# A one-core ViT block with a mixture of experts: the token step rearranged, scatters behind the normalising, four adds under way

## The reference

```python
h = einsum('bnd,ed->bne', patches(x), W) + b             # 768 -> 192
q, k, v = split(LN(h) @ W_attn + b_attn)                 # 12 heads of 16, rotary q and k
h = h + softmax(causal(q k^T / 4)) v @ W_proj + b_proj   # over the 16 tokens of an image
z = LN(h)
t = z * rsqrt(mean(z * z) + 1e-5) * norm_scale           # rmsnorm of the layer-normed row
g = t @ gate_w.T + gate_b                                # 16 experts, the best 4
w = softmax(top4(g))
y = sum over the 4: w_e * (swiglu(t @ W1_e + b1_e) @ W2_e + b2_e)   # inner width 384
return h + z + y
```

## Time and profile before

| what | value |
| --- | --- |
| device time, three runs | 524.96 us median (522.0 to 531.15) |
| profiled execution | 521.43 us, its span 519.6 us |
| PE busy in the span | 437.7 us (84%) |
| ACT, DVE, POOL busy | 311.0, 303.9, 257.2 us |
| mean granted clock of TensorE | 0.927 |
| moved by DMA | 49.73 MB, mean 96 GB/s |

### The profile page before, as it was taken

How to read it: one execution, slowest core, us unless ns; L and a number is a source line. 1 busy time by engine, 2 the same in 40 slices (tenths; PEclk the granted TensorE clock), 3 DMA queues, 4 the chain that set the end, 5 groups by cost and what they waited for, 6 DMA issues and landing times. The chain is left out here.

```text
span 519.6 us, 14443 instructions
## 1 busy us (share of the span) xinstructions
PE 437.7 (84%) x3867; PEld 388.2 (75%) x3868; DVE 303.9 (58%) x1048; ACT 311.0 (60%) x832; POOL 257.2 (50%) x302
## 2 busy tenths in 40 slices
PE   3788887797777758339999999999999999999970
PEld 2666765675566546229999999999999999999970
DVE  0466977878787666614555555555555555555550
ACT  1257656666665563217776767677766767777730
POOL 1124476667676666730334445345453644454443
PEclk9899999989999775559999999999999999999995
DMA  7995554555565111223333534434434443342332
GB/s 213 218 228 163 148 159 146 151 169 159 169 179 154 54 50 50 77 87 96 49 49 50 83 57 73 68 56 64 63 56 64 64 64 58 55 65 32 32 32 23
DMA packets 42107, 49.73 MB, mean 96 GB/s; under 512 B 6387, under 2 KB 33507, under 8 KB 42052
## 3 DMA queue, kind: packets, MB, share of 16 engines
q1 hardware_dynamic: 27604, 34.35, 25.2%
q0 software_dynamic: 14448, 14.72, 18.6%
HBM read 30.82 MB, written 18.23 MB: 94 GB/s over the span
## 5 line engine op out<-in xcount | busy, mean ns | idle before, releaser
L1200 POOL DMA_INDIRECT out_rows<-x_sb,row_to x79 | 125.9, 1593 | 161.6 <-DMA out_rows<-x_sb,row_to 78.5
L589 PE MATMUL bank<-rT,w_now 128*128 128x128 f32 x948 | 124.0, 281 | 0.3 <-ACT rT L634 0.3
L589 PEld LDWEIGHTS bank<-rT,w_now 128*128 128x128 f32 x948 | 115.1, 193 | 5.2 <-ACT rT L634 0.5
L634 ACT ACTIVATE w_now<-w_sb 128x1158 f32 x79 | 92.4, 1170 | 22.4 <-issue 17.2
L724 ACT ACTIVATE k_spread<-bank,w_now 128x128 f32<-128x128 f32 x237 | 70.1, 372 | 58.2 <-PE bank L597 52.5
L1077 DVE TENSOR_TENSOR v_sb<-bank,w_now 128x384 f32<-128x384 f32 x79 | 44.1, 558 | 85.5 <-PE bank L597 60.2
L611 PE MATMUL bank<-w_sb,p_spread 128*128 x474 | 83.9, 327 | 0.1
L1144 POOL DMA_INDIRECT routed_rows<-packet,row_i x64 | 64.7, 1012 | 24.1 <-issue 22.2
L611 PEld LDWEIGHTS bank<-w_sb,p_spread 128*128 128x128 f32 x474 | 76.1, 190 | 0.5 <-issue 0.4
L1090 DVE SCALAR_TENSOR_TENSOR p_spread<-k_spread,v_sb 128x384 f32<-128x384 f32 x79 | 44.1, 558 | 36.7 <-ACT k_spread L724 28.2
L597 PE MATMUL bank<-rT,w_now 64*128 64x128 f32 x948 | 64.2, 281 | 0.0
(11 more groups left out here) (182 smaller groups left out, 598.8 us busy)
## 6 DMA issues: line engine op xcount, KB each, us to landing
x_sb<-patches SPq DMA_DIRECT2D x16, 384.0 KB, 3.6
w_sb<-w SPq DMA_DIRECT2D x32, 192.0 KB
w_sb<-w SPq DMA_DIRECT2D x16, 288.0 KB
w_sb<-w SPq DMA_DIRECT2D x64, 48.0 KB
wtok_sb<-routed_rows SPq DMA_DIRECT2D x25, 106.0 KB, 2.0
routed_rows<-zero_row SPq DMA_DIRECT2D x17, 106.0 KB
out_rows<-h SPq DMA_DIRECT2D x16, 96.0 KB
out_rows<-x_sb,row_to POOLq DMA_INDIRECT x79
```

The lines of the kernel that those rows point to most:

```text
L589: last = mm(dst[:, c * P:(c + 1) * P], w[:, a:a + P], t[:, part, :], start=(start and c == 0), stop=(not start and c == ICH - 1))
L634: return nc.scalar.activation(dst, src, ACT.Copy)
L1200: G.indirect_dma_start(out=out, out_offset=bass.IndirectOffsetOnAxis(ap=row_to[:, b % NY:b % NY + 1].bitcast(U32), axis=0), in_=y_out[b % ...
```

## The change

**Norm.** rmsnorm of a layer-normed row depends on the variance v alone: z = (h1 - m) / sqrt(v + e), and z * rsqrt(v/(v+e) + e) = (h1 - m) * (v + e'), to the power -1/2, times a constant, with e' = e*e/(1+e). POOL computes both roots at once from two columns (`attn_roots`); DVE's `norm2` writes the scaled row straight into the packet. The norm scale and the constant move out of the rows: into the gate weights once at the start, and into a per-partition scale with which ACT moves the turned rows of the expert stage (two instructions of 128 columns in place of one of 256). The residual becomes one ACT instruction (h1 * gain + shift), gain and shift two one-column instructions of DVE. The square and its sum, `norm3`, the packet copy, the copies of weights and of two index tiles go.

**Order.** PE turns xn, q, k and the packet first, and embedding stands behind the projection; bias and v product come before values, which are last. On POOL the scatters of a tile are issued one step later, right behind `normalise`, ahead of the roots. On DVE `embed_add`, its statistics and xn come late in the step, rope products and qk early.

**Buffers.** Four packets instead of two. Four adds of the expert stage may be under way: an add waits for those of j - 1 to j - 3 only where an expert's border lies between, told by two rows of the table.

The core of the diff:

```diff
@@ def owed_to
-                return 16 * (j // 2 + 1) if j >= 0 else 0
-            return (j - buf % 2) * 8 + 16
+                return 16 * (j // ADDS + 1) if j >= 0 else 0
+            return (j - buf % ADDS) * (16 // ADDS) + 16
@@ tensor, start of the first step
+                    for c in range(2):
+                        a = c * (DIM - P)
+                        mm(ps_ns[:, c:c + 1], ns_line[:, a:a + P], ident[0:1, 0:1], start=True, stop=True)
...
@@ scalar
-                copy(rT[buf % 2][:], ps_rT[buf % 2]).then_inc(r["rT_ready"], 1)
+                for c in range(2):
+                    last = nc.scalar.activation(rT[buf % 2][:, c, :], ps_rT[buf % 2][:, c, :], ACT.Copy,
+                                                scale=ns_row[:, c:c + 1])
+                last.then_inc(r["rT_ready"], 1)
...
+                    act.wait_ge(s["shift_ready"], t + 1)
+                    nc.scalar.activation(h0[:, t, :], h1[:], ACT.Identity, bias=shift[:], scale=gain[:]
+                                         ).then_inc(s["base_ready"], 1)
@@ vector, norm2
-                dve.wait_ge(s["rstd2_ready"], t + 1)
-                wait(dve, s["ssq_ready"], t)
-                V.tensor_scalar(x2[:], h1[:], mv2[:, 0:1], rstd2[:], ALU.subtract, ALU.mult
-                                ).then_inc(s["x2_ready"], 1)
+                packed = packet[t % PACKETS]
+                dve.wait_ge(s["roots_ready"], t + 1)
+                wait(dve, scattered[t % PACKETS], rows_out(t, t % PACKETS))
+                V.tensor_scalar(packed[:, 0:DIM], h1[:], mv2[:, 0:1], roots[:, 0:1], ALU.subtract, ALU.mult
+                                ).then_inc(s["t_row_ready"], 1)
@@ gpsimd, step
+                late = n - STAGES
                 if tile(3) is not None:
                     normalise(tile(3))
+                if 0 <= late < TILES - 1:
+                    scatter(late, 0, TOPK)
+                if tile(4) is not None:
+                    attn_roots(tile(4))
                 if tile(0) is not None:
-                    inverse_root(tile(0), mv1[:, 1:2], 1.0, "mv1_ready", ve1, "ve1_ready", rstd1, "xn_ready",
-                                 "rstd1_ready")
...
+                    embed_root(tile(0))
+                if tile(6) == TILES - 1:
+                    scatter(tile(6), 0, TOPK)
@@ gpsimd, add
-                    wait(pool, added[b % 2], owed_to(j - 2, b))
...
+                        if b % ADDS > 0:
+                            owed = pool.value_load(table_i[0:1, 2, bass.ds(j, 1)], min_val=32, max_val=16 * SLOTS)
+                        if b % ADDS < ADDS - 1:
+                            owed_wrap = pool.value_load(table_i[0:1, 3, bass.ds(j, 1)], min_val=16, max_val=16 * SLOTS)
+                        for i in range(1, ADDS):
+                            pool.wait_ge(added[(b - i) % ADDS], owed if b % ADDS >= i else owed_wrap)
```

More of the change, by code:

```diff
@@ L95, in shape_constants @@
     put("token", p[:, None] + P * np.arange(TILES)[None, :])
[L96 removed]
+    put("owed", 16 * (p[:, None] // ADDS))
     return c
@@ L160, in build @@
         h1 = sb("h1", [P, DIM])
[L161 to L165, removed]
+        stats2, mv2 = sb("stats2", [P, 6]), sb("mv2", [P, 2])
+        eps2, power2, ve2, roots = (sb(n, [P, 2]) for n in ("eps2", "power2", "ve2", "roots"))
+        gain, shift = sb("gain", [P, 1]), sb("shift", [P, 1])
+        packet = [sb(f"packet{i}", [P, ROW]) for i in range(PACKETS)]
         tT = sb("tT", [HALF + 1, 2, P])
-        top_v, top_i, top_f = sb("top_v", [P, 8]), sb("top_i", [P, 8], U32), sb("top_f", [P, TOPK])
+        top_v, top_i = sb("top_v", [P, 8]), sb("top_i", [P, 8], U32)
         top_d, top_e, top_w = sb("top_d", [P, TOPK]), sb("top_e", [P, TOPK]), sb("top_w", [P, TOPK])
@@ L666, in step @@
             def step(tile, seen, n):
-                if tile(6) is not None:
-                    t, buf = tile(6), (n - 6) % 2
-                    act.wait_ge(s["t_row_ready"], t + 1)
-                    wait(act, scattered[buf], rows_out(t, buf))
-                    copy(packet[buf][:, 0:DIM], t_row[buf][:]).then_inc(s["packed"], 1)
+                if tile(3) is not None:
+                    t = tile(3)
+                    act.wait_ge(s["sc2_ready"], t + 1)
+                    wait(act, s["p_pair_ready"], 2 * t)
+                    wait(act, s["rsum_ready"], t)
+                    nc.scalar.activation(prob[:], sc2[:], ACT.Exp).then_inc(s["prob_ready"], 1)
                 if tile(1) is not None:
@@ L1034, in tab @@
                 made[0] += 1
-            column = [of_tile[:, i:i + 1] for i in range(10)]
+            column = [of_tile[:, i:i + 1] for i in range(11)]
             dve.wait_ge(counted, 1)
@@ L1147, in residual @@
-            def residual(t):
-                pool.wait_ge(s["x2_ready"], t + 1)
-                G.tensor_tensor(base[:, bass.ds(t, 1), :].rearrange("p a d -> p (a d)"), h1[:], x2[:], ALU.add
-                                ).then_inc(s["base_ready"], 1)
+                for k in range(k0, k1):
+                    G.indirect_dma_start(out=routed, out_offset=bass.IndirectOffsetOnAxis(
+                        ap=row_i[t % 2][:, k:k + 1].bitcast(U32), axis=0),
+                        in_=packet[buf][:], in_offset=None).then_inc(scattered[buf], 16)
```

297 lines of the change are left out of this document (141 added, 156 removed).

## The result

The changed kernel takes 538.34 us (median of 6 runs, 537.12 to 540.88), the kernel before beside it 525.74 us (6 runs, 522.0 to 531.15). The ratio on record is 1.0284 with a 95% interval of 1.0247 to 1.0321 (the two medians alone give 1.024): slower, and beyond the forecast 530 us. In the two profiled executions the span goes from 519.6 to 535.9 us, 16.3 us more.

The account below looks back on a forecast made before the run. PE bounds the expert stage, waits between engines the token stage. Profiled 521.4 us, +8 token stage, -2.5 adds gave 527; on the level of the runs' median 530 us, with 515 to 543 to hold 8 in 10.

Parts of the forecast that it names:

- The circle through POOL and DVE: Steady token step, from one normalising to the next: 12.8 us against 11.74, nine steps +9.5 us.
- gap: POOL's wait between normalising and the first scatter in a steady step, taken as 0.55 us.
- Start and six steps, +1: Token stage's start and six steps before scatters: second and third step longer, later ones shorter, +1 us, bounds -4 and +5.
- Drain -3: End of token stage, step 17's sc2 to the last scatter's end: 32.0 us against 34.8, so -3.
- Expert stage 0: Expert stage: rT moved in two halves costs ACT +0.25 us per tile, hidden by PE, so 0 us.
- Adds -2.5: Last adds of the expert stage start earlier with four under way: -2.6 us, or -1.5 if table reads cost POOL time.
- PE's clock: Slower rival: PE idles before xn, drops to half clock and bounds the token step; about 545 us, chance 0.11.
- Late reports: Slower rival: PE reports late under every scatter, token step about 14 us; about 540 us, chance 0.10.
- the even rival: Ramp and drain give more than counted: -4 bound, step of 12.2, -4 at the end; 517 us, chance 0.14.
- +0.5: Token steps 16 and 17, which lack embedding and its statistics, at 11.9 us: +0.5 us.
- The rule weighed in the prediction: GpSimd can't write descriptors while VectorE holds their shared port; scatters beside rope products could all be long, nine times +1.4.

Follow-up runs that it names:

- the runs with three and two scatters ahead: Changed kernel with three, or two, of POOL's four scatters ahead of the roots of h1, the rest behind: 524.25 us (ratio 1.0016) and 512.64 us (0.9987).
- The early order in three steps: Changed kernel with scatters parted by the roots, ACT's code moved on, and embedding early in steps 0 to 2: 508.76 us, ratio 0.9712; 512.99 without the early order.
- the run with two: Changed kernel with two adds under way in place of four: 540.29 us, ratio 1.0282 to the kernel before.
- the kernel before, padded: Kernel before with 16 no-effect waits added in ACT's loop body over the expert tiles: 513.71 us, ratio 1.0019.
- moved on: Changed kernel with 60 no-effect waits at the start of ACT's program: 536.13 us, ratio 1.02.
- the first group: Four follow-up runs on one chip, where the kernel before took 512.81 us.
- the kernel before with POOL's waits added: Kernel before with 24 no-effect waits added in POOL's loop body over the adds: 512.82 us, ratio 1.0024.
- the second group: Four follow-up runs on another chip, where the kernel before took 525.53 us.
- early embedding: Changed kernel with the embedding of steps 0 to 5 put back early on PE, DVE and POOL: 535.82 us, ratio 1.0476 to the kernel before.
- scatters held back: Three-step early-embedding kernel, with POOL's last four scatters waiting until the table of expert tiles is worked out: 510.39 us, ratio 0.9747.

## Why the prediction failed, point by point

The direction was right (slower), the size not: 12.6 us where 5 were forecast. The time lies inside the stated range of 515 to 543, but by sums that went wrong in both directions. The step that failed is the term for the start, set at +1 us where +7.4 was measured; the code loaded at ACT's turns and the table behind the last scatters were not priced at all.

1. *The circle through POOL and DVE*: right in kind, and shown by the runs with three and two scatters ahead. By its items: normalising 0.98 (1.1 said), gap 0.17 (0.55 said), four scatters 4.93 (5.0), roots 1.03 (0.98), norm2 to sc2 3.19 (3.3), sc2 to the next normalising 1.87 (1.86): 12.2, where 12.8 stood. The gap was mis-sized; the row with 0.17 was the right one, since packets and row numbers of the tile before are ready long before. Nine steps cost 5.6 and not 9.5, and the gap alone is 3.4 us of that.
2. *Start and six steps, +1*: the step that failed most, +7.4. The prediction put the second and third step 2 us each longer, for DVE's embed_add behind the rope products, and expected the later ones to be shorter. It followed DVE's order and not PE's: the embedding stands behind a qk product which waits for the xn of the tile before, and xn for that tile's embedding. Steps 1 and 2 became one chain of 10.1 and 8.5 us, against 5.0 and 4.9 (distances of embed_add), with PE at half clock from 13.0 to 23.2. The early order in three steps took 5.9 us back by the two profiles, 4.2 by the medians. The 7.4 is the difference of two profiles too; over all traces with either start (seven and three) sc2 of step 6 comes at 71.1 and 65.0 us on the mean, 6.0 apart, which is still far above +1.
3. *Drain -3*: the last scatter ended 31.6 us after sc2 of step 17, 3.2 us sooner than before, as said. But the load of expert rows waits for the table as well. Before, table and last scatter were ready almost together (227.2 and 226.6), a wait that the prediction did not price; now the table is 4.6 us behind the scatters (240.7 and 236.1): its small steps on DVE (23, before 22) take 9.1 us in place of 4.3, beside scatters in one unbroken row, and the gain is gone.
4. *Expert stage 0*: right for what was weighed, since the pairs last 6.80 us as before and the halves of rT lie beside PE. The 4.5 us are the two stalls where code is loaded at the turns of ACT's loop (9.6 and 10.1 us, less what the pairs behind make up), which no step of the prediction looked at.
5. *Adds -2.5*: -1.9 in the trace, 2.1 by the trace of the run with two.
6. *Rivals*: PE's clock fell (0.87) and cost nothing in the steady step, since project stays ahead of the scatters: of two steps in a row (sc2 to sc2, from 120.66 us) the first has a granted clock of 0.98 and lasts 12.20 us, the second 0.78 and 12.18. Late reports did not make the step, but they go with the slow table. The sum of the even rival is off: with 9 x 0.46 us of the steps, +0.5, -4 at the start, -4 in the drain and -2.5 it gives 515.5, not 517.

The rule weighed in the prediction changed next to nothing: the scatters last 956 to 1197 ns, median 962, in the changed kernel, as in the earlier trace rows, though the first of a step now lies beside the rope products (1.06 us in the step shown, the others 0.96 to 1.02). That the rope products hold the port was assumed; no row shows it.

Adding the misses to the forecast: start +6.4, expert stage +4.5, drain +2.3, first load to y_out +0.9, adds +0.6, steady steps -3.9, in all 10.8 us, against 8.3 us by the medians; the rest is that the profiled executions lie at other distances from their medians. What lengthened the 0.9 us was not tried.

## What to carry to other kernels

Follow an edited order on every engine once for the steady step and once for the first steps, where a late instruction has nothing to hide behind. Put long work that nobody waits for (here four scatters of 1.27 us) behind the short work that somebody does, cut to fit the gaps. After an edit that lengthens a looped program, look at the turns of the loop in the trace and at the packets of the code queue there; here 60 instructions ahead of the loop took the two long stalls away.

## What the runs showed of the hardware

**Code loaded at a loop's turn depends on where the loop lies.** In ACT's program a body of 276 instructions turned without a stall where 718 stand ahead of it (the kernel before, padded) or 733 (moved on), and with two long stalls where 673 do (the changed kernel); the kernel before has 260 behind 702 and no stall. These are counts of the built programs. The change altered both numbers, and a body of 276 alone did no harm. The Trainium skill, Runtime: NRT & Kernel Launch, section Instruction fetch mechanics, says that a taken branch to a block outside those held forces a load of it. The trace agrees in that code is loaded at such a turn. The page gives blocks of 16 KiB; here the packets of this queue are of 8 KB (30 packets, 0.25 MB in the whole kernel before), and whether two of them make a block was not measured, nor how many blocks ACT holds.

**Reports come late beside scatters, on some chips and not on others.** A report is late when an engine starts well after the record of what it waits for has ended. Each chip was seen on one occasion, so it may be the occasion as well. In the earlier trace rows yT starts 4.2 us after PE's record of values ends. The same code on the chip of the first group (the kernel before with POOL's waits added): values end at 150.49 + 0.86 = 151.35, and yT starts at once.

```profile
150.49 0.86 PE L480 MATMUL bank<-p_spread,v_sb 128*32 128x128 f32 x24 [1.06 <-ACT p_spread L634]
...
151.41 0.48 ACT L634 ACTIVATE yT<-bank 128x384 f32<-128x384 f32 x1
```

Its nine steady steps last 10.84 us on the mean there, against 11.66 on the first profile's chip; with the two steps behind them that is 10.8 of the 13 us between the kernel before on the two. DVE's own reports are late too. The same step of the table, changed kernel in the second group and early embedding in the first:

```profile
234.71 0.16 DVE L1027 SCALAR_TENSOR_TENSOR of_tile<-of_tile 128x1 f32<-128x1 f32 x1 [1.79 <-remote]
```

```profile
228.69 0.16 DVE L1041 SCALAR_TENSOR_TENSOR of_tile<-of_tile 128x1 f32<-128x1 f32 x1
```

The whole table takes 10.1 us in the one and 2.5 in the other. With scatters held back on a chip of the late kind it quickened at once, so scatters are likely a part of the cause; what differs between the chips stays open. It also moves the ratio: the changed kernel's step is 12.3 us on either kind (12.25 on the mean in the kernel with six early embeddings, whose steady steps are the same, where reports are timely), so the change costs 2.6 to 2.8 per cent where the kernel before suffers from late reports, and with timely ones a version that differs from the changed kernel only in the order of its first six steps was 4.8 per cent behind.
